# A Mamba and mixture-of-experts layer on one core: the experts one after the other with the second product split by hidden part, and tables by token for the last two experts

## The reference

```
x1  = layernorm(x + mamba(x))
out = layernorm(x1 + moe(x1))          # (v - mean) / sqrt(var + 1e-5), no scale or bias
```

## Time and profile before

| What | Value |
|---|---|
| Time, median of 3 runs | 414.87 us (414.5 to 415.67) |
| The profiled execution: its time, its span | 416.17 us, 414.4 us |
| Busy in the span: PE, DVE, ACT, POOL | 69%, 69%, 45%, 64% |
| Mean granted clock of PE | 0.836 of full speed |

### The profile page before, as it was taken

How to read it: one execution, slowest core, us unless ns; L and a number is a source line. 1 busy time by engine, 2 the same in 40 slices (tenths; PEclk the granted TensorE clock), 3 DMA queues, 4 the chain that set the end, 5 groups by cost and what they waited for, 6 DMA issues and landing times. The chain is left out here.

```text
span 414.4 us, 4635 instructions
## 1 busy us (share of the span) xinstructions
PE 284.9 (69%) x1388; PEld 197.9 (48%) x1402; DVE 287.9 (69%) x447; ACT 188.3 (45%) x363; POOL 264.1 (64%) x226
## 2 busy tenths in 40 slices
PE   7757676647887765974564896764389999998100
PEld 4425344423774442763442452232377888887100
DVE  1959999978999989899999899996001112111246
ACT  4593764576554665565544345423114222332005
POOL 3503889863868987989989875795700444456640
PEclk9989998978969668888555699899589999999755
DMA  7050375542112331231132311001142333221173
GB/s 220 0 206 2 113 222 148 179 161 103 58 57 78 120 120 65 67 122 52 54 106 70 120 59 52 0 13 40 46 135 59 103 115 112 93 84 38 38 202 101
DMA packets 30264, 38.68 MB, mean 93 GB/s; under 512 B 3590, under 2 KB 21707, under 8 KB 30240
## 3 DMA queue, kind: packets, MB, share of 16 engines
q1 hardware_dynamic: 26960, 33.32, 25.7%
q0 software_dynamic: 2304, 4.24, 3.0%
q10 hardware_dynamic: 976, 0.83, 0.6%
HBM read 28.01 MB, written 10.69 MB: 93 GB/s over the span
## 5 line engine op out<-in xcount | busy, mean ns | idle before, releaser
L1150 POOL TENSOR_TENSOR product<-state,c_wide 128x1024 f32<-128x1024 f32 x64 | 149.6, 2341 | 59.8 <-DVE state L1348 40.5
L868 ACT ACTIVATE psum<-dt,a_neg 128x512 f32<-128x512 f32 x128 | 88.0, 689 | 109.0 <-DVE state L1348 109.0
L558 PE MATMUL psum<-ident,product 128*128 128x128 f32 x384 | 62.8, 318 | 40.4 <-POOL product L1150 39.8
L1348 DVE TENSOR_TENSOR_SCAN state<-psum,carry,drive 128x512 f32<-128x512 f32 x64 | 79.7, 1269 | 4.4 <-ACT psum L868 4.2
L558 PEld LDWEIGHTS psum<-ident,product 128*128 128x128 f32 x384 | 51.7, 163 | 60.2 <-POOL product L1150 56.5
L1332 DVE TENSOR_TENSOR drive<-dtu,psum 128x1024 f32<-128x1024 f32 x64 | 76.6, 1197 | 4.8 <-remote 2.8
L1348 DVE TENSOR_TENSOR_SCAN state<-psum,drive 128x512 f32<-128x512 f32 x64 | 75.3, 1207 | 2.5 <-ACT psum L868 2.3
L1270 POOL DMA_INDIRECT result_rows<-state,result_at x40 | 38.9, 971 | 53.1 <-DVE state L1573 40.4
L1225 POOL DMA_INDIRECT slot_rows<-sent,scatter_at x32 | 32.5, 1015 | 10.4 <-issue 6.8
L736 PE MATMUL psum<-product,fc_sb 128*128 128x320 f32 x128 | 36.2, 436 | 2.1 <-DVE product L1554 1.1
L553 PE MATMUL psum<-product,ident 128*128 128x512 f32 x60 | 30.1, 631 | 9.4 <-POOL product L1150 9.2
(11 more groups left out here) (218 smaller groups left out, 410.1 us busy)
## 6 DMA issues: line engine op xcount, KB each, us to landing
c_wide<-c_rows SPq DMA_DIRECT2D x32, 512.0 KB, 3.8
slot_rows<-blank SPq DMA_DIRECT2D x8, 325.0 KB, 4.6
c_wide<-slot_rows SPq DMA_DIRECT2D x8, 325.0 KB, 3.2
result_rows<-zeros SPq DMA_DIRECT2D x8, 256.0 KB, 5.0
fc_sb<-in_c_fc SPq DMA_DIRECT2D x8, 256.0 KB
proj_sb<-in_c_proj SPq DMA_DIRECT2D x8, 256.0 KB
c_wide<-result_rows SPq DMA_DIRECT2D x8, 256.0 KB, 5.0
x_tok<-in_x SPq DMA_DIRECT2D x4, 256.0 KB, 6.1
```

The lines of the kernel that those rows point to most:

```text
L558: last = nc.tensor.matmul(y_part(j, d), product[:, i, d, j * P:(j + 1) * P], ident[:, :], is_transpose=True, start=False, stop=True, skip_ ...
L868: nc.scalar.activation(psum[:, A_BANK + d, :], dt[:, q % 2, d, :], ACT.Exp, scale=a_neg[:, n:n + 1]).then_inc(decay_ready, 1)
L1150: nc.gpsimd.tensor_tensor(product[:, U % PRODUCTS, channels, :], state[:, U % RING, channels, :], wide, ALU.mult).then_inc(product_ready, 1)
L1348: nc.vector.tensor_tensor_scan(state[:, U % RING, d, :], psum[:, A_BANK + d, :], drive[:, U % 2, d, :], before, ALU.mult, ALU.add).then_in ...
```

## The change

- PE takes the experts strictly one after the other: second(e), first(e+1), turn(e+2). `second_layer` runs over the hidden parts h outside and the slot tiles s inside, and waits for one part at a time, so that five sums are open at once in banks 6 and 7. For expert 7 only, `last_second_layer` has a bank for each tile, takes parts 0 to 2 of two tiles first and then the rest.
- `center_proj` (DVE, new): for each expert the mean over the 128 output channels is taken out of `proj_sb` (a reduction and one scalar_tensor_tensor), so that each result row has mean zero. x1 has mean zero as well, so that the last layernorm needs no mean.
- A new table `late_rows` in HBM, 2 x 2,048 rows by token: expert 6 writes to the first half, expert 7 to the second. SP clears it with 8 transfers of 256 KB, in the scan at load_c steps 12 to 19.
- Behind the five scatters of expert 5, SP loads `result_rows`, first the first choice, then the second (8 transfers). Behind expert 6's scatters it loads the first half of `late_rows` (4), behind expert 7's the second half (4).
- DVE adds in the order: x1 and the first choice (4 groups), then expert 7's evictions, then the second choice, then expert 6's table, and last expert 7's. POOL adds nothing any more.
- Variance by squares: of each group's four tiles ACT squares two and DVE two, each with a running sum; DVE adds eps, POOL raises to the power -0.5, and ACT (two tiles) and DVE (one instruction for two tiles) scale.

The core of the diff:

```diff
+        late_rows = nc.dram_tensor("late_rows", [2 * TOKENS, D_MODEL], F32, kind="Internal").ap()
...
+        last_results = product[:, 2:4, :, :].rearrange("p a b (j d) -> p (a b j) d", d=D_MODEL)
...
-        LAST_BANKS = [[0, 1, 6, 7, 2], [3, 4, 5, 0, 1]]
+        LAST_BANKS = [6, 7, 0, 1, 2]
...
+                if C_SLOTS + CLEARS <= m < C_SLOTS + 2 * CLEARS:
...
+                    sp.dma_start(blank_late[m - C_SLOTS - CLEARS], zeros[:, :]).then_inc(late_cleared, 16)
...
-            for i in range(2):
-                sp.wait_ge(results_sent[i], 16 * SLOT_TILES * PAIRS)
+            sp.wait_ge(rows_turned, N_EXP)
+            sp.wait_ge(tags_copied, N_EXP)
+            sp.wait_ge(results_sent[0], 16 * SLOT_TILES * (PAIRS - 1))
+            sp.wait_ge(results_sent[1], 16 * SLOT_TILES * (PAIRS - 1))
             in_order = result_rows.rearrange("(k j p) d -> p (k j) d", k=TOP_K, p=P)
-            for g, k in ((0, 0), (1, 0), (0, 1), (2, 0), (1, 1), (3, 0), (2, 1), (3, 1)):
...
+            for k in range(TOP_K):
+                for g in range(GROUPS):
+                    at = slice(k * TILES + TPC * g, k * TILES + TPC * (g + 1))
+                    sp.dma_start(results[:, at, :], in_order[:, at, :]).then_inc(results_loaded[k][g], 16)
+            late_in_order = late_rows.rearrange("(i j p) d -> p i j d", i=2, p=P)
+            sp.wait_ge(late_sent[0], 16 * SLOT_TILES)
             for g in range(GROUPS):
...
+                at = slice(TPC * g, TPC * (g + 1))
+                sp.wait_ge(results_added, g + 1)
+                sp.dma_start(results[:, at, :], late_in_order[:, 0, at, :]).then_inc(late_loaded[0][g], 16)
+            sp.wait_ge(late_sent[1], 16 * SLOT_TILES)
+            for g in range(GROUPS):
+                at = slice(TPC * g, TPC * (g + 1))
+                sp.dma_start(last_results[:, at, :], late_in_order[:, 1, at, :]).then_inc(late_loaded[1][g], 16)
...
+            def second_layer(e):
+                i = e % 2
+                pe.wait_ge(proj_centered, e + 1)
+                if e:
                     pe.wait_ge(rows_out_ready, e)
...
+                for h in range(HT):
+                    pe.wait_ge(hidden_ready, HT * e + h + 1)
+                    for s in range(SLOT_TILES):
+                        last = nc.tensor.matmul(psum[:, 6 + s // TPC, s % TPC * P:(s % TPC + 1) * P], hidden[i][:, h, s * P:(s + 1) * P],
+                                                proj_sb[:, i, h, :], start=(h == 0 and s % TPC == 0), stop=(h == HT - 1), skip_group_check=True)
+                last.then_inc(proj_done, 1)
...
+                for s in range(2):
+                    for h in range(HT - 1):
+                        part(s, h)
+                for s in range(2):
+                    part(s, HT - 1).then_inc(last_proj_done, 1)
+                for s in range(2, SLOT_TILES):
                     for h in range(HT):
...
+            turn_rows(0)
+            first_layer(0)
+            turn_rows(1)
+            for e in range(N_EXP - 1):
+                second_layer(e)
+                first_layer(e + 1)
+                if e + 2 < N_EXP:
+                    turn_rows(e + 2)
+            last_second_layer()
...
+                nc.gpsimd.tensor_tensor(rstd[:, tiles], variance[:, tiles], minus_half[:, :], ALU.pow).then_inc(rstd2_ready, 1)
...
+            for e in range(2):
+                center_proj(e)
+                copy_turned(e)
+            for e in range(2, N_EXP):
+                copy_results(e - 2)
+                copy_turned(e)
+                center_proj(e)
+            copy_results(N_EXP - 2)
...
+                nc.vector.tensor_tensor(final[:, tiles, :], x1[:, tiles, :], results[:, tiles, :], ALU.add).then_inc(results_added, 1)
+            copy_results(N_EXP - 1)
...
+            def add_last(g):
...
+                nc.vector.tensor_tensor(final[:, tiles, :], final[:, tiles, :], last_results[:, tiles, :], ALU.add).then_inc(all_added, 1)
...
+                for j in range(TPC // 2):
...
+            def vary(g):
...
+                nc.vector.tensor_scalar(variance[:, tiles], sum_squares2[:, tiles], EPS, None, ALU.add).then_inc(variance_ready, 1)
...
+            def scale(g):
...
+            add_last(0)
+            vary(0)
+            for g in range(GROUPS):
+                if g + 1 < GROUPS:
+                    add_last(g + 1)
+                    vary(g + 1)
+                scale(g)
```

More of the change, by code:

```diff
@@ L1053, in _, with activate_hidden @@
             act.preload_act_table(ACT.Gelu)
-            def activate_hidden(g, i):
-                e = 2 * g + i
-                first = isinstance(g, int) and g == 0
-                if not first:
+            def activate_hidden(e):
+                if e >= 2:
                     act.wait_ge(proj_done, e - 1)
@@ L1071, in inverse_root @@
-            def inverse_root(tiles, ready, value, done):
-                act.wait_ge(ready, value)
-                nc.scalar.activation(log_var[:, tiles], moments[:, tiles, 1], ACT.Ln, scale=-2.0).then_inc(act_step, 1)
-                act.wait_ge(act_step, step.up())
-                nc.scalar.activation(rstd[:, tiles], log_var[:, tiles], ACT.Exp, scale=-0.5).then_inc(done, 1)
-            def normalize(rows, g, done, count=TPC):
-                for j in range(TPC * g, TPC * g + count):
-                    nc.scalar.activation(rows[:, j, :], rows[:, j, :], ACT.Identity, scale=rstd[:, j:j + 1],
-                                         bias=shift[:, j:j + 1]).then_inc(done, 1)
+            for e in range(N_EXP):
+                activate_hidden(e)
@@ new lines, in square_results, with normalize @@
+            def square_results(g):
+                act.wait_ge(all_added, g + 1)
+                if g >= 2:
+                    act.wait_ge(early_squared, TPC // 2 * (g - 1))
+                for j in range(TPC // 2):
+                    t = TPC * g + j
+                    nc.scalar.activation(squares[:, g % 2 * TPC // 2 + j, :], final[:, t, :], ACT.Square, scale=D_MODEL ** -0.5,
+                                         accum_out=sum_squares2[:, t:t + 1]).then_inc(early_squared, 1)
+            def normalize(g):
+                act.wait_ge(rstd2_ready, g + 1)
+                for t in range(TPC * g, TPC * g + TPC // 2):
+                    nc.scalar.activation(final[:, t, :], final[:, t, :], ACT.Identity, scale=rstd[:, t:t + 1]).then_inc(out_ready, 1)
@@ L1091, in _ @@
+            normalize(GROUPS - 1)
         @block.gpsimd
@@ L1602, in _ @@
[L1602 to L1606 removed]
+                dve.wait_ge(results_added, g + 1)
+                nc.vector.tensor_tensor(final[:, tiles, :], final[:, tiles, :], results[:, TILES + TPC * g:TILES + TPC * (g + 1), :],
+                                        ALU.add).then_inc(results_added, 1)
```

242 lines of the change are left out of this document (106 added, 136 removed).

## The result

| | before | after |
|---|---|---|
| Time, median | 415.38 us (6 runs, 414.5 to 416.44) | 411.87 us (6 runs, 410.41 to 412.79) |
| The profiled execution: its time, its span | 416.17, 414.4 us | 412.02, 410.3 us |
| From the start of the last scan to the end of the span | 128.6 us | 123.65 us |

The ratio of after to before is 0.9915, 95% interval 0.9894 to 0.9936: faster by 0.85%, where 2.4% was forecast, and 411.87 us is outside the range of 402 to 409. Timed again on another chip the ratio was 0.9958, 0.9928 to 0.9988. The span was forecast at 404.4 us and is 410.3: 5.9 us have to be found.

The account below looks back on a forecast made before the run. PE was taken to bound the experts, then POOL's scatter queue, then an unoverlapped end. Some 4.7 us up to the last scatter and 5.3 from the end made 10.0, from a median of 414.87 to 404.9 us; range 402 to 409 (0.82).

Parts of the forecast that it names:

- PE's stretch: PE in the experts: reordered without pauses, second products staying 4.47 us, second(7) ending at 382.2 where the last product ended 385.3.
- rival 3: PE's second products: open sums cost what L637 shows, 3.3 us more, giving 408.2; chance 0.05.
- rival 4: PE's second products: open sums or lost clock make the kernel slower than before, up to 441 at half clock; chance 0.05.
- Landing and SP's reaction take 2.31: Behind expert 5's last scatter: 2.31 us until SP's first load of `result_rows`, putting the loads at 373.2.
- So it costs 0.4: POOL's queue: expert 7's evictions, behind the first-choice adds, are ready at 382.0, 0.4 us behind POOL's own 381.6.
- I add 5 x 0.04 = 0.2 (at most 1.5): Expert 7's five scatters: slowed beside DVE's work from 0.97 to a median 1.007 us each, 0.2 us in all.
- The store takes 2.9: End of the program: 2.9 us from the last instruction at 401.5 to the span's end at 404.4.
- I take 0.3: Final layernorm: POOL's power for the last group adds 0.3 us, bounded between 0.235 and 1.15; hidden for groups 0 to 2.
- 5.3 from the end: Behind the last scatter: some 5.3 of the 10.0 us gain, from a shorter final pipeline and no wait for second-choice loads.
- rival 1: Loads beside scatters: twelve loads share engines with ten scatters, land 3 us later, sums not hidden; 2.8 us, 407.7; chance 0.07.
- Rival 2: POOL's queue: expert 7's evictions come late, as expert 6's did, 2.3 us behind; 407.2 to 409; chance 0.12.
- Rivals 5 and 6: Whole kernel: more gain than counted, 401 to 402.5, chance 0.09; or no effect, 414 to 416, chance 0.02.

## Why the prediction was wrong, step by step

**PE's stretch: right.** The terms 4.47, 4.35 and 0.54 hold (now 4.47, 4.31 to 4.35, 0.55) and there is no pause; the last product ends at 383.20, forecast 382.2 plus the 1.1 by which all starts later. Open sums cost nothing (rival 3 falls), and the clock is 1.00 (rival 4 falls). `center_proj` takes 0.68 + 0.69 = 1.37 us per expert, forecast 1.4, and is hidden: DVE's idle time ahead of an eviction goes from 3.49 to 2.17.

**"Landing and SP's reaction take 2.31": failed for expert 5.** It took 3.90, because PE's instruction fetch fell into it. The figure itself was nearly right: 2.27 for expert 7, and 2.53 for expert 5 with the fetch moved, of which 0.21 is the fifth scatter's length of 1.18 under `center_proj`. Cost 1.6 us: the loads start that much later, and with them the adds ahead of expert 7's evictions.

**"So it costs 0.4": mis-sized.** The mechanism, evictions behind adds behind loads, was named; the wait measured 1.34 us beyond the usual 0.30, for the reason above.

**"I add 5 x 0.04 = 0.2 (at most 1.5)": mis-sized by kind.** I priced the adds' effect on scatters by the median of the earlier trace rows. Their median was the wrong measure: the effect depends on which kind of DVE instruction runs when the scatter starts, and four such adds back to back make it 1.26 us in a single scatter. The earlier trace rows had it in its longest: the scatter of 1278 ns starts under a DVE product of two SBUF tiles (L1512, 278.22 to 280.22), most of the others under instructions that read PSUM.

**"The store takes 2.9": failed, the largest term.** 2.9 was the distance from DVE's last instruction to the end as long as SP's stores set the end. The change put POOL's last instruction at 404.06, and the program can't end before 5.98 us after that. The trace of before had it, and I didn't read it: a DRAIN of 7.19 us on POOL, hidden with 4.5 us to spare (409.65 against 414.20). Cost 2.6 us, and shown from both sides (-2.9 and +2.4). No rival had it.

**"I take 0.3" for the power: mis-sized.** It measured 1.11 for the last group, near the upper bound of 1.15. With the hand-over it is 0.6 us of the end by the root on ACT; the 9.0 us from landing to last instruction came out at 8.9, so the other parts of that sum were some 0.9 too high. The 12.1 us in the bracket behind "5.3 from the end" don't follow from the prediction's own rows, which give 9.0 from landing to last instruction where 14.4 were; the sum doesn't use them.

**"5.3 from the end", and what the change's tables are worth: wrong in its balance.** From last scatter to end the kernel after is 2.8 us shorter (22.46 to 19.69), and with the root on ACT, so without the DRAIN at the end, 6.3 (to 16.17). Of these, 3.2 to 3.8 are there without tables too (18.66 and 19.29), and 2.5 to 3.0 are the early sums. But the early sums cost 3.1 to 3.2 in POOL's queue, which the prediction had at 0.6. With that repaired (evictions between the adds) the sum is 119.13 us, against 119.20 and 119.82 without tables, and 404.49 against 405.6 us by time, with intervals that overlap: at best about 1 us for them. Without tables and with the root on ACT the gain is 8.8 to 9.4 us by the traces, of the forecast's 10.0: POOL's last scatter starts 5.6 us earlier (106.17 to 100.54), 3.4 of it because PE's last product ends earlier (99.54 to 96.17 us after the last scan) and the rest because the scatters of the last two experts stand without the gaps of the earlier trace rows. The shorter end holds several changes at once (squares, no Newton step, DVE's adds), and no run takes them apart.

**Rivals.** Of rival 1 (loads late, evictions wait with them, last adds slip) the first half came, by the landing and not by its reason of twelve loads beside ten scatters: the eight loads went out in 5.12 us, 4.91 before, and the fourth was taken up 6.3 us after the first issue, 6.4 before. The last adds, its 2.8 us, didn't slip: they end at 392.30, 3.6 us ahead of the next load. What the loads do hold up are the scatters beside them: expert 6's table is loaded from 385.81 on, 4.6 us after its fifth scatter, where 382.6 was forecast; here that is hidden. Rival 2 named the right place with another cause: no tile is taken late once its turn comes. Rivals 5 and 6 fall.

Left open: why the runs with the split undone spread over 6 us, what POOL does in its 6 us of DRAIN, and where the 1.5 to 3.4 us are by which the medians gained less than the stretch behind the last scan.

## What to carry to other kernels

Look at each engine's DRAIN at the end of a trace before moving an instruction to POOL late in a program: here the program can't end until 6 us after POOL's last one, which is free only as long as the stores end later. Before putting DVE work beside POOL's scatters, look which of it reads two operands from SBUF; one of them in PSUM, or the order of the queue changed, keeps scatters at their pitch. Work that is moved under a busy stretch to shorten the end is worth only what it doesn't cost there: compare both lengths, up to the last scatter and behind it, not the sum of what was hidden.

## What the runs showed of the hardware

- POOL's closing DRAIN ended 5.96 to 6.06 us after the end of POOL's last instruction in 14 of 14 traces, whether that was a scatter, an add, a power or a memset of 0.1 us.
- A scatter's issue on POOL (0.97 us) that starts under a DVE instruction with two f32 operands in SBUF ended 0.84 to 0.85 us after the end of that one or of a later one in the same run: 2.23 to 2.24 us under four adds in four traces, 1.18 under one. With one operand in PSUM it stayed at 0.97.
- An instruction fetch of 16 KB by PE, one packet of 0.88 to 1.5 us, came with a landing of 3.7 to 4.2 us for a scatter of 64 KB issued 1.4 to 1.7 us ahead of it (10 traces), against 2.5 in the two traces where the fetch fell elsewhere.
- Loads of 1 MB beside the last scatters made their landing 3.84 to 4.05 us instead of 2.32.
- A power of 128 x 4 values on POOL took 1.11 to 1.36 us; its other arithmetic on such tiles took 0.19 to 0.24.
- Five sums open at once in two PSUM banks cost nothing: 4.47 us for 40 f32 instructions, as with one at a time, at clock 1.00.
